# Norms and turns of queries and keys dealt out tile by tile beneath the projections of a causal attention

## The reference, cut to what matters

```python
hx = _layernorm(x, ln_g, ln_b)
q = (hx @ Wq).reshape(b, n, h, dh).transpose(0, 2, 1, 3)   # h = 8 heads of dh = 64
k = (hx @ Wk).reshape(b, n, h, dh).transpose(0, 2, 1, 3)
v = (hx @ Wv).reshape(b, n, h, dh).transpose(0, 2, 1, 3)
q = _l2norm(q) * scale * qn_g        # x / sqrt(sum(x*x over dh) + 1e-12)
k = _l2norm(k) * scale * kn_g
scores = jnp.einsum('bhqd,bhkd->bhqk', q, k) * dh ** (-0.5)
scores = jnp.where(causal, scores, jnp.finfo(scores.dtype).min)
attn = jax.nn.softmax(scores, axis=-1)
```

## Time and profile before

| what | value |
|---|---|
| median of 3 runs | 2567.64 us (2566.18 to 2568.13) |
| the profiled execution | 2563.54 us, its span 2561.7 us |
| busy over the span | PE 2222.7 us, DVE 1346.4 us, POOL 798.7 us, ACT 709.9 us |
| the stage's projections, tile to tile | 10.73 us |
| from the last projection's end to the next stage | 1481.57 to 1514.71 us |

### The profile page before, as it was taken

The page is one execution under the profiler, slowest core; times in us unless marked ns, Lnnn a source line. Parts: engine busy times, 40 slices in busy tenths (PEclk is TensorE's granted clock), DMA queues, the critical chain, the costliest instruction groups (busy, mean ns, idle before and its releaser), DMA issues.

```text
span 2561.7 us, 31158 instructions
## 1 busy us (share of the span) xinstructions
PE 2222.7 (87%) x11374; PEld 1274.3 (50%) x11374; DVE 1346.4 (53%) x4100; ACT 709.9 (28%) x1573; POOL 798.7 (31%) x552
## 2 busy tenths in 40 slices
PE   1999984998965999997899989988999989898974
PEld 0455552443322444445663457667876653455543
DVE  5455676778963666662114264431122242279996
ACT  3111121221003444442121155653211120133442
POOL 2018888887875565660000000000000000012222
PEclk9998887998987999998999979998899999999987
DMA  9982222222236666653001020001100022000000
GB/s 362 419 339 3 3 3 19 4 4 20 3 35 149 179 171 169 171 142 146 1 1 49 1 107 1 1 1 76 58 1 1 1 58 78 0 1 9 9 9 17
DMA packets 90266, 180.62 MB, mean 71 GB/s; under 512 B 65109, under 2 KB 66070, under 8 KB 74135
## 3 DMA queue, kind: packets, MB, share of 16 engines
q1 hardware_dynamic: 44367, 176.77, 21.3%
q0 software_dynamic: 45072, 1.46, 5.4%
q10 hardware_dynamic: 674, 0.39, 0.1%
HBM read 110.27 MB, written 68.31 MB: 70 GB/s over the span
## 4 chain that ended last, share of the span: by engine, by line
PE 59%; DVE 18%; POOL 10%; ACT 5%; issue 5%; DMA 3%; SPq 0%; DVEq 0%; ACTq 0%; POOLq 0%
PE banks L192 16%; POOL edge_table L506 8%; PE banks L2002 6%; PE banks L2029 5%; PE banks L1435 3%; PE banks L1258 3%; PE banks L1271 2%; DMA edge_table<-arena 2%; PE banks L1813 2%; PE banks L1840 2%; PE banks L1827 2%; PE banks L328 2%; PE banks L186 2%; POOL arena L1215 2%; PE banks L1862 2%
## 5 line engine op out<-in xcount | busy, mean ns | idle before, releaser
L192 PE MATMUL banks<-arena 128*125 128x512 f32 (+1 forms) x1280 | 582.9, 604 | 38.7 <-ACT arena L2531 29.1
L506 POOL DMA_INDIRECT edge_table<-arena x313 | 491.9, 1572 | 249.2 <-DMA edge_table<-arena 158.6
L192 PEld LDWEIGHTS banks<-arena 128*125 128x125 f32 x1280 | 239.3, 195 | 320.6 <-issue 270.5
L1183 DVE TENSOR_TENSOR arena<-banks,arena 125x500 f32<-125x500 f32 x200 | 208.5, 1051 | 162.5 <-ACT banks L1235 158.8
L1215 POOL TENSOR_TENSOR arena<-arena 125x500 f32<-125x500 f32 x180 | 222.6, 1247 | 149.4 <-DVE arena L1183 143.5
L1258 PE MATMUL banks<-arena 64*125 64x250 f32 x800 | 142.6, 434 | 64.8 <-DVE arena L1183 58.2
L2342 POOL MEMSET arena<- 128x1024 f32 x2 | 1.8, 951 | 581.6 <-DVEq L143 581.6
L1950 DVE SCALAR_TENSOR_TENSOR arena<-banks,arena 125x512 f32<-125x512 f32 x80 | 60.1, 751 | 203.7 <-PE banks L2029 203.7
L1235 ACT ACTIVATE banks<-banks 125x500 f32<-125x500 f32 x200 | 114.6, 573 | 173.1 <-PE banks L1261 172.7
L186 PE MATMUL banks<-arena 125*128 125x125 f32 x560 | 92.0, 302 | 69.9 <-DVE arena L180 50.3
L2002 PEld LDWEIGHTS banks<-arena 128*128 128x128 f32 x1280 | 145.7, 194 | 6.9 <-issue 6.8
(11 more groups left out here) (324 smaller groups left out, 3481.2 us busy)
## 6 DMA issues: line engine op xcount, KB each, us to landing
edge_table<-arena SPq DMA_DIRECT2D x24, 2250.0 KB, 36.2
arena<-edge_table SPq DMA_DIRECT2D x50, 984.4 KB
arena<-L_ffn_W SPq DMA_DIRECT2D x4, 2048.0 KB, 8.1
arena<-edge_table SPq DMA_DIRECT2D x50, 114.3 KB
adjacency<-arena SPq DMA_DIRECT2D x50, 109.4 KB
arena<-adjacency SPq DMA_DIRECT2D x10, 546.9 KB
edge_table<-arena POOLq DMA_INDIRECT x313, 3.0
arena<-x SPq DMA_DIRECT2D x1, 2240.0 KB
```

The costliest lines, as they stand in the source:

```text
L192: last = nc.tensor.matmul(dst, xT[:, i, :], w[:, i, 0:n], start=(i == 0), stop=(i == k - 1))
L506: pool.indirect_dma_start(d["table"], bass.IndirectOffsetOnAxis(ap=cell[0:EP, c:c + 1].bitcast(U32), axis=0), vals[0:EP, c * ROW:(c + 1) * ...
L1183: nc.vector.tensor_tensor(P_g[n % PRING][0:TP, :].rearrange("p (e n) -> p e n", e=2), two_scores(n), ring[(c * TILES + b) % RING][0:TP, :, ...
```

## The change

The norms and turns of tile t - 1 now stand inside iteration t of the projection loop, and only those of the last tile are left behind it. On VectorE `squares_summed(t - 1)` stands ahead of the Q copy of tile t and `rows_normalized(t - 1)` behind it; each works on the tile's own 16 columns, so that the plus, the reciprocal and the Newton step are now ten small ones of each in place of one wide one. On ScalarE the loop runs squares of t - 1, copies of the turned rows of t - 2, z of t + 1, root of t - 1. On TensorE the eight turns of tile t - 1 stand behind the V projection of tile t, and write banks 5 and 6 (the last tile's banks 0 and 1). Since the folded products use banks 5 and 6 too, they now also wait for the copies of tile 8. No instruction of another stage is changed, and the amount of arithmetic is the same but for the small steps.

```diff
--- before.py
+++ after.py
@@ -1556,41 +1556,55 @@
                     dve.wait_ge(z_turned, Z_FFN + t)
                 normalize(z_c[0:TP, :], XN[0:TP, t, :], t).then_inc(z_rows, 1)
 
+            def norms(m, t):
+                return m[0:TP, 2 * HEADS * t:2 * HEADS * (t + 1)]
+
+            def squares_summed(t):
+                for which in range(2):
+                    dve.wait_ge(c_sq, 2 * t + which + 1)
+                    n = 2 * t + which
+                    nc.vector.tensor_reduce(ss[0:TP, n * HEADS:(n + 1) * HEADS],
+                                            sq_c[which][0:TP, :].rearrange("p (h n) -> p h n", h=HEADS),
+                                            AX_X, ALU.add).then_inc(c_ss, 1)
+                dve.wait_ge(c_ss, 3 * t + 2)
+                nc.vector.tensor_scalar(norms(sv, t), norms(ss, t), 1e-12, None, ALU.add).then_inc(c_ss, 1)
+
+            def rows_normalized(t):
+                dve.wait_ge(c_ss, 3 * t + 3)
+                dve.wait_ge(c_sr, t + 1)
+                link(dve, nc.vector.reciprocal(norms(sr, t), norms(sa, t)))
+
+                link(dve, nc.vector.tensor_tensor(norms(ss, t), norms(sv, t), norms(sr, t), ALU.mult))
+                link(dve, nc.vector.tensor_tensor(norms(ss, t), norms(ss, t), norms(sr, t), ALU.mult))
+                link(dve, nc.vector.tensor_scalar(norms(ss, t), norms(ss, t), -0.5, 1.5, ALU.mult, ALU.add))
+                link(dve, nc.vector.tensor_tensor(norms(sr, t), norms(sr, t), norms(ss, t), ALU.mult))
+                for which in range(2):
+                    row = (Q_f, K_f)[which][0:TP, t, :].rearrange("p (h n) -> p h n", h=HEADS)
+                    c = (2 * t + which) * HEADS
+                    nc.vector.tensor_tensor(row, row, sr[0:TP, c:c + HEADS].unsqueeze(2)
+                                            .to_broadcast([TP, HEADS, DH]), ALU.mult).then_inc(c_n, 1)
+
             z(0)
             for t in range(TILES):
                 if t + 1 < TILES:
                     z(t + 1)
+                if t >= 1:
+                    squares_summed(t - 1)
                 for j, row in enumerate((Q_f[0:TP, t, :], K_f[0:TP, t, :], V_f[0:TP, t, :])):
                     dve.wait_ge(c_proj, 3 * t + j + 1)
                     nc.vector.tensor_copy(row, bank(2 + j)[0:TP, :]).then_inc(c_ev, 1)
-
-            for n in range(2 * TILES):
-                dve.wait_ge(c_sq, n + 1)
-                nc.vector.tensor_reduce(ss[0:TP, n * HEADS:(n + 1) * HEADS],
-                                        sq_c[n % 2][0:TP, :].rearrange("p (h n) -> p h n", h=HEADS),
-                                        AX_X, ALU.add).then_inc(c_ss, 1)
-            dve.wait_ge(c_ss, 2 * TILES)
-            nc.vector.tensor_scalar(sv[0:TP, :], ss[0:TP, :], 1e-12, None, ALU.add).then_inc(c_ss, 1)
-            dve.wait_ge(c_ss, 2 * TILES + 1)
-            dve.wait_ge(c_sr, 1)
-            link(dve, nc.vector.reciprocal(sr[0:TP, :], sa[0:TP, :]))
-
-            link(dve, nc.vector.tensor_tensor(ss[0:TP, :], sv[0:TP, :], sr[0:TP, :], ALU.mult))
-            link(dve, nc.vector.tensor_tensor(ss[0:TP, :], ss[0:TP, :], sr[0:TP, :], ALU.mult))
-            link(dve, nc.vector.tensor_scalar(ss[0:TP, :], ss[0:TP, :], -0.5, 1.5, ALU.mult, ALU.add))
-            link(dve, nc.vector.tensor_tensor(sr[0:TP, :], sr[0:TP, :], ss[0:TP, :], ALU.mult))
-            for n in range(2 * TILES):
-                t, which = divmod(n, 2)
-                row = (Q_f, K_f)[which][0:TP, t, :].rearrange("p (h n) -> p h n", h=HEADS)
-                nc.vector.tensor_tensor(row, row, sr[0:TP, n * HEADS:(n + 1) * HEADS].unsqueeze(2)
-                                        .to_broadcast([TP, HEADS, DH]), ALU.mult).then_inc(c_n, 1)
+                    if j == 0 and t >= 1:
+                        rows_normalized(t - 1)
+
+            squares_summed(TILES - 1)
+            rows_normalized(TILES - 1)
             leave_stage(dve, "DVE")
 
         def ffn_act(act):
             ln_stats_act(act)
             ln_stats_act(act)
             act.wait_ge(s_wc, 16 * 8)
-            for t in range(TILES):
+            def zT(t):
                 act.wait_ge(z_turned, Z_FFN + t + 1)
                 if t >= 2:
                     act.wait_ge(c_proj, 3 * t - 3)
@@ -1599,28 +1613,57 @@
                                                 ACT.Identity, scale=lg_f[:, k:k + 1],
                                                 bias=lg_f[:, KC + k:KC + k + 1])
                 last.then_inc(z_cols, 1)
-                if t == 0:
-                    fold_dense_act(act)
-            for n in range(2 * TILES):
-                t, which = divmod(n, 2)
-                act.wait_ge(c_ev, 3 * t + 1 + which)
-                if n >= 2:
-                    act.wait_ge(c_ss, n - 1)
-                nc.scalar.activation(sq_c[n % 2][0:TP, :], (Q_f, K_f)[which][0:TP, t, :],
-                                     ACT.Square).then_inc(c_sq, 1)
-            act.wait_ge(c_ss, 2 * TILES + 1)
-            nc.scalar.activation(sa[0:TP, :], sv[0:TP, :], ACT.Sqrt).then_inc(c_sr, 1)
+
+            def squares(t):
+                for which in range(2):
+                    act.wait_ge(c_ev, 3 * t + 1 + which)
+                    if t >= 1:
+                        act.wait_ge(c_ss, 3 * (t - 1) + which + 1)
+                    nc.scalar.activation(sq_c[which][0:TP, :], (Q_f, K_f)[which][0:TP, t, :],
+                                         ACT.Square).then_inc(c_sq, 1)
+
+            def deviations(t):
+                act.wait_ge(c_ss, 3 * t + 3)
+                c = slice(2 * HEADS * t, 2 * HEADS * (t + 1))
+                nc.scalar.activation(sa[0:TP, c], sv[0:TP, c], ACT.Sqrt).then_inc(c_sr, 1)
+
+            def turned(t):
+                for which in range(2):
+                    act.wait_ge(c_tqk, 2 * t + which + 1)
+                    nc.scalar.activation((qT_f, kT_f)[which][:, :, tok(t)], chunks(qk_bank(t, which), TP), ACT.Copy,
+                                         scale=gain[:, 2 * which:2 * which + 1]).then_inc(c_qkT, 1)
+
+            zT(0)
+            fold_dense_act(act)
+            for t in range(TILES):
+                if t >= 1:
+                    squares(t - 1)
+                if t >= 2:
+                    turned(t - 2)
+                if t + 1 < TILES:
+                    zT(t + 1)
+                if t >= 1:
+                    deviations(t - 1)
+            squares(TILES - 1)
+            turned(TILES - 2)
+            deviations(TILES - 1)
             fold_query_act(act)
-            for n in range(2 * TILES):
-                t, which = divmod(n, 2)
-                act.wait_ge(c_tqk, n + 1)
-                nc.scalar.activation((qT_f, kT_f)[which][:, :, tok(t)], chunks(bank(n % 4)[:, :], TP), ACT.Copy,
-                                     scale=gain[:, 2 * which:2 * which + 1]).then_inc(c_qkT, 1)
+            turned(TILES - 1)
             leave_stage(act, "ACT")
+
+        def qk_bank(t, which):
+            return bank(5 + which if t < TILES - 1 else which)
 
         def ffn_pe(pe):
             fold_dense_pe(pe)
             pe.wait_ge(s_wc, 16 * 8)
+
+            def turn_qk(t):
+                for which in range(2):
+                    pe.wait_ge(c_n, 2 * t + which + 1)
+                    if 1 <= t < TILES - 1:
+                        pe.wait_ge(c_qkT, 2 * (t - 1) + which + 1)
+                    transpose_tile(chunks(qk_bank(t, which), TP), (Q_f, K_f)[which][0:TP, t, :]).then_inc(c_tqk, 1)
 
             def turn(t):
                 pe.wait_ge(z_rows, Z_FFN + t + 1)
@@ -1639,14 +1682,12 @@
                     project(bank(2 + j)[0:TP, :], zT_c[t % 2], w).then_inc(c_proj, 1)
                     if j == 0 and t + 1 < TILES:
                         turn(t + 1)
+                if t >= 1:
+                    turn_qk(t - 1)
             pe.wait_ge(c_ev, 3 * TILES)
+            pe.wait_ge(c_qkT, 2 * TILES - 2)
             fold_query_pe(pe)
-            for n in range(2 * TILES):
-                t, which = divmod(n, 2)
-                pe.wait_ge(c_n, n + 1)
-                if n >= 4:
-                    pe.wait_ge(c_qkT, n - 3)
-                transpose_tile(chunks(bank(n % 4)[:, :], TP), (Q_f, K_f)[which][0:TP, t, :]).then_inc(c_tqk, 1)
+            turn_qk(TILES - 1)
             leave_stage(pe, "PE")
 
 
```

## The result

| | before | changed |
|---|---|---|
| median, first comparison (4 runs each) | 2566.91 us | 2547.95 us |
| ratio, 95% interval | | 0.9923 (0.9909 to 0.9937) |
| ratio in a second comparison (6 runs against 23) | | 0.9914 (0.9897 to 0.9931) |
| span of the profiled execution | 2561.7 us | 2541.3 us |

The account below looks back on a forecast made before the run. TensorE was taken to bound the projection loop, the norms on VectorE and ScalarE the tail. -14.8 us (tail) + 8.0 (loop) = -6.8 us, from a median of 2567.64 to 2560.8 us; range 2556 to 2565.5 us.

Parts of the forecast that it names:

- The stage: The edited attention stage: tail gain less loop cost, -6.8 us; by the turns alone -7.9 to -5.7.
- The loop: Projection loop: eight tiles' turns added on TensorE at 1.00 us each cost 8.0 us, bounds 6.9 to 9.1.
- The tail: From the last projection's end to the last copy: 18.3 us in place of 33.07, a gain of 14.8 us.
- No stall: In the loop, scaled rows would be ready before TensorE's turns need them, with 2.6 us of slack, at least 1.5.
- no cost of the stores: At the stage's end, later stores of the products would delay the next stage's first exponential by nothing, at worst 1.5 us.
- norms hidden beneath the products: In the tail, tile 9's norms, at most 6.0 us, lie under 14.1 us of folded products; priced at nothing.
- Rival C: In the projection loop, the clock falls once per tile: slower, +8.5 us, 2576 us; chance 3%.
- the rule on turns: Skill's rule that transposes do not engage full clock, putting the loop's clock at risk; the prediction said the trace disagrees.
- The step that failed: Start of the next stage: TensorE's idle time and low-clock stretches (9.1 and 14.7 us) stay as before, plus or minus 2 us.
- Rival D: The next stage starts with a warm clock: 4 to 6 us more gain, 2555 to 2557 us; chance 6%.
- The other term of the clock: Folded products in the tail: the clock falls as before, so they keep 14.10 us, within 11.5 and 16 us.
- all the stated bounds together: Limits given for the turns (-7.9 to -5.7 us), the products (11.5 to 16 us) and the next stage's clock (2 us).

Follow-up runs that it names:

- e1: The kernel before, run again with no edit; ratio to before 1.0006 (0.9993 to 1.0020).
- e4: The kernel before with 12 extra fp32 products on TensorE, issued before it waits for the other engines at the stage's end; ratio to before 0.9995.
- e2: The changed kernel, run again with no edit; ratio to before 0.9914 (0.9897 to 0.9931).

## Why the prediction was wrong

**The stage.** Right. The loop cost 8 x 0.86 = 6.9 us, the lower bound (8.0 taken). The tail gave 14.9 us: 18.2 us against 33.1. Together 8.0 us. The profiles say the same where like stands against like: 143.3 against 135.3 us with the fall at the first projections (before and e1, changed), 141.8 against 133.8 us without it (e4, e2). No stall, no cost of the stores, norms hidden beneath the products, as priced.

**Rival C and the rule on turns.** With twelve turns among 24 projection instructions per tile the granted clock was 1.00 over 105 us of the loop. By itself that says little, as the projections are 10.30 of 11.59 us. Together with the rise amid turns in the earlier trace rows, this case gives no support to what the Trainium skill (TensorE: Matmul & The Clock Gate, Part 4: PE-mode transpose) says of transposes and the full clock.

**The step that failed** is the last of the change's parts: "TensorE stops about 3.1 us ahead of it before and about as long now, so I keep that too, plus or minus 2 us." The idle time did stay (3.09 us before L1854). But what decides the causal stage's clock is not the idle time ahead of it. At half clock its first tiles may or may not regain the full clock; before they did so after 25 us, in the changed kernel after 16, and three later falls went too. That is 20.4 us less at half clock and 8.8 us of time (287.1 against 278.3), more than the stage itself gave, where 2 us at most were allowed for. Rival D named the place and 4 to 6 us; both its size and its 6% were too small. It took a third to a half of the half-clock time as lying on the chain, and only of the first 24 us; here 8.8 us are 0.86 of what 20.4 us could give. The other term of the clock was sized rightly: the products took 14.05 us, 14.10 forecast. But in before the clock fell amid the narrow products, 2.9 us behind their start, and not after them. Even all the stated bounds together (-7.9 by the turns, -2.6 in the products, -2 in the next stage) make only 12.5 us of gain. The earlier trace rows held the warning: 24 us at half clock, with TensorE busy for most of them (6.08 of 10.30 us, then 34.86 of 35.00), are a stretch where a small shift can change much.

**The rest.** Means of the two profiles of each kernel: 1.3 us earlier at the start of the stage, 8.7 us in it, 8.8 us in the causal stage, 2.1 us behind it (761.8 against 759.7 us), 20.9 in all, beside 19.0 and 19.6 us of the medians. 0.7 of the 8.7 us are the fall at the first projections that e2 did not have. The first and the last come from stages without any edit, and the rows show no gain of the change in them. Behind the causal stage before took 759.8 us in its first profile, as the changed kernel did twice (759.7); e1 took 763.7, with 7.3 us more at half clock there. Ahead of the stage one execution differs from another of the same kernel by as much as 5.3 us (1368.0 and 1373.3 us in the changed one). So part of the 19 us may be scatter of what the change does not touch.

**Open.** What brings the work into step with the instants at which the clock can change. The Trainium skill (TensorE: Matmul & The Clock Gate, Part 1: The HAM clock gate) calls the chip's watch over TensorE's work free-running. Within one execution the clock record agrees: in each of the fourteen profiles all falls and rises, from the kernel's first to its last, keep one even beat to within 0.01 us. Against the work, however, the beat did not lie at random: the first fall in the causal stage came within 0.1 us of the same piece of work in two executions of before and in two of the changed kernel, though the stage's own start had moved by 0.9 and 3.8 us against the span's. No run here tells why. Nor is it shown which piece of the causal stage makes the difference between a rise at 16 and at 25 us.

## What to carry to other kernels

Where TensorE is the bound, work on it that moves out of a tail into the loop costs its full time, and the tail is what remains on the longest of the other engines: the tail came out within 0.2 us by adding durations from rows, the loop at the lower of its two bounds. But a stage that starts after a pause and is at half clock while TensorE is busy reacts to when it starts; give its clock a range of its own, up to half of its half-clock time (here it was 0.44 us for each us at half clock), and test a gain there by a kernel that only shifts the start. Profile a kernel more than once before you read a few microseconds of such a stage. Where the products are on the chain, keep narrow ones from standing in one block behind a wait.

## What was not expected of the hardware

- Wasted work made the kernel faster: four copies on VectorE, 1.4 us, gave 0.47% (medians 2554.81 us against 2567.35), for the most part by the clock of a stage that they do not touch (279.3 us against 287.1).
- 32 narrow instructions (8 columns) in a row let the clock fall while TensorE counted as busy; the same ones in blocks of eight among wide ones did not: 14.05 against 10.73 us.
- Two executions of one kernel, with 0.1 us of difference in where the clock's instants fell, took 278.3 and 284.0 us for one stage.
